# First layer's grouped attention: key blocks stored and loaded by SyncE, both halves in one transfer, and the first turn's operands fetched early

## The reference

```
q = (h @ Wq.T)                              # 32 heads of 128
k_r0 = h @ Wkr.T                            # the rotary part of 8 key heads
c_kv = h @ Wdk.T                            # latents, 512 wide
k_c = c_kv @ Wupk.T ; v = c_kv @ Wupv.T     # the other key part, the values
q, k = q*cos + rotate_half(q)*sin, k*cos + rotate_half(k)*sin
scores = q @ k.T / sqrt(128), causal ; attn = softmax(scores)
out = (attn @ v) @ Wo.T                     # 4 query heads share a key head
```

## Time and profile before

| what | value |
|---|---|
| median of 3 runs | 2360.93 us (2348.55 to 2364.01) |
| the profiled execution | 2363.39 us, its span 2361.7 us |
| granted TensorE clock, mean | 0.959 of full |
| PE busy | 2153.1 us, 91% of the span |
| attn0b, key/value stage after the latents | 405.84 to 516.46 us |
| attn0b, first scores | 540.36 us |

### The profile page before, as it was taken

The page is one execution under the profiler, slowest core; times in us unless marked ns, Lnnn a source line. Parts: engine busy times, 40 slices in busy tenths (PEclk is TensorE's granted clock), DMA queues, the critical chain, the costliest instruction groups (busy, mean ns, idle before and its releaser), DMA issues. The chain is left out here.

```text
span 2361.7 us, 33423 instructions
## 1 busy us (share of the span) xinstructions
PE 2153.1 (91%) x11504; PEld 1480.1 (63%) x11504; DVE 1414.9 (60%) x2599; ACT 1093.5 (46%) x2639; POOL 840.2 (36%) x1062
## 2 busy tenths in 40 slices
PE   6999998887999999999997869999999986899988
PEld 4344366665777777777775656777777664554457
DVE  5777575416566556565663645666666555757756
ACT  4666653214444444444443535555555533325553
POOL 2000000534444444443442025555544412346621
PEclk9899999997999999999999979999999997989999
DMA  2000023651111111111110244433333201543310
GB/s 89 1 1 1 1 76 111 139 118 52 41 54 32 41 54 32 41 32 32 36 50 31 67 103 108 108 91 100 92 98 78 78 23 53 160 95 68 71 34 36
DMA packets 112542, 149.18 MB, mean 63 GB/s; under 512 B 39588, under 2 KB 52516, under 8 KB 110200
## 3 DMA queue, kind: packets, MB, share of 16 engines
q1 hardware_dynamic: 64376, 108.77, 16.3%
q0 software_dynamic: 48000, 38.28, 7.1%
HBM read 86.07 MB, written 27.26 MB: 48 GB/s over the span
## 5 line engine op out<-in xcount | busy, mean ns | idle before, releaser
L1842 POOL TENSOR_TENSOR attn0b_probs<-attn0b_probs,attn0b_recip 128x128 f32<-128x128 f32 (+3 forms) x256 | 192.5, 772 | 223.4 <-DVE attn0b_recip L2081 223.2
L2473 POOL TENSOR_TENSOR attn1a_probs<-attn1a_probs,attn1a_recip 128x128 f32<-128x128 f32 (+3 forms) x256 | 179.2, 721 | 232.9 <-DVE attn1a_recip L2656 232.3
L2529 ACT ACTIVATE attn1a_probs<-attn1a_scores,attn1a_negmax 128x128 f32<-128x128 f32 (+3 forms) x256 | 132.8, 524 | 174.5 <-DVE attn1a_negmax L2642 173.3
L1948 ACT ACTIVATE attn0b_probs<-attn0b_scores,attn0b_negmax 128x128 f32<-128x128 f32 (+3 forms) x256 | 132.8, 524 | 149.5 <-DVE attn0b_negmax L2074 148.3
L1956 ACT ACTIVATE attn0b_probsT<-attn0b_turned 128x128 f32<-128x128 f32 (+3 forms) x128 | 56.0, 438 | 245.7 <-PE attn0b_turned L2222 245.3
L2235 PE MATMUL attn0b_out<-attn0b_probsT,attn0b_v_now 128*128 128x512 f32 x320 | 155.6, 617 | 11.8 <-DVE attn0b_probsT L2088 11.8
L1468 DVE TENSOR_REDUCE attn0a_negmax<-attn0a_by_query 128x2 f32<-128x1024 f32 x128 | 152.3, 1219 | 21.3 <-PE attn0a_by_query L1555 21.3
L2642 DVE TENSOR_REDUCE attn1a_negmax<-attn1a_scores 128x2 f32<-128x256 f32 (+3 forms) x128 | 105.5, 824 | 70.6 <-PE attn1a_scores L2831 70.6
L2074 DVE TENSOR_REDUCE attn0b_negmax<-attn0b_scores 128x2 f32<-128x256 f32 (+3 forms) x128 | 104.8, 819 | 46.5 <-PE attn0b_scores L2211 46.5
L37 PE MATMUL attn0b_aux<-attn0b_wo_hi,attn0b_oT_hi 128*128 128x512 f32 x256 | 126.4, 494 | 1.4 <-DVE attn0b_oT_lo L2092 1.4
L2843 PE MATMUL attn1a_turned<-ident_f,attn1a_probs 128*128 128x128 f32 x640 | 115.8, 279 | 8.6 <-DVE attn1a_probsT L2650 7.2
(11 more groups left out here) (510 smaller groups left out, 6115.0 us busy)
## 6 DMA issues: line engine op xcount, KB each, us to landing
pre<-in_b_o SPq DMA_DIRECT2D x16, 1024.0 KB, 5.3
attn1a_qT<-attn1a_stage SPq DMA_DIRECT2D x128, 128.0 KB, 2.4
attn1a_qT<-attn1a_stage SPq DMA_DIRECT2D x64, 256.0 KB, 3.8
pre<-in_b_q SPq DMA_DIRECT2D x8, 1024.0 KB, 6.4
pre<-in_b_kv SPq DMA_DIRECT2D x5, 1024.0 KB, 5.8
attn0b_vals<-attn0b_v_out SPq DMA_DIRECT2D x16, 256.0 KB, 4.0
attn0b_keys_hi<-attn0b_part_hi POOLq DMA_DIRECT2D x32, 128.0 KB, 5.1
attn0b_keys_lo<-attn0b_part_lo POOLq DMA_DIRECT2D x32, 128.0 KB, 7.7
```

Of the source, the lines that this page charges most:

```text
L1842: pool.tensor_tensor(x, x, recip[:, r % 2, e:e + 1].broadcast_to([P, (qt + 1) * P]), ALU.mult).then_inc(s_scaled, 1)
L1948: act.activation(probs[:, r % 2, e, 0:width], scores[r % 2][:, e, 0:width], ACT.Exp, bias=negmax[:, r % 2, e:e + 1], accum_out=sums[:, r % ...
L2473: pool.tensor_tensor(x, x, recip[:, r % DEEP, e:e + 1].broadcast_to([P, (qt + 1) * P]), ALU.mult).then_inc(s_scaled, 1)
L2529: act.activation(probs[:, r % DEEP, e, 0:width], scores[r % 2][:, e, 0:width], ACT.Exp, bias=negmax[:, r % 2, e:e + 1], accum_out=sums[:, ...
```

## The change

Keys are kept in device memory in one tensor with both halves next to each other; a key part lies in one buffer `part`, of which there are three (`SLOTS`). SP stores it, hi and lo together, in two transfers in place of four, from 64 partitions each; the target is two heads by 64 rows by 512. SP also loads the keys of each turn, with two transfers in place of four. POOL issues none of these any more. SP loads the values of turn 0 after V10 and the keys of turn 0 after V12, inside the key/value stage, and the buffers are laid out anew so that these targets are free by then. The output weights of turn 0 are split at N4, not at `at == 1`. Weights 3 are split one block earlier, at R7. At `at == 0` ACT and DVE wait for all key stores too.

```diff
--- before.py
+++ after.py
     LEAD = 5
+    SLOTS = 3
     FIRST, LAST = -LEAD, TILES_ALL + 1
...
-        keys_hi, keys_lo = [dram(f"keys_{k}", (TURNS, 2, 2, 32, BATCH * SEQ), F32R) for k in ("hi", "lo")]
+        keys = dram("keys", (TURNS, 2, 2, 32, 2, BATCH * SEQ), F32)
             take_sb = lambda name, shape, dt=F32: first.enter_context(nc.sbuf_tensor(f"{prefix}_{name}", shape, dt))
+            part = take_sb("part", [P, SLOTS, 2, SEQ], F32R)
+            v_out = take_sb("v_out", [P, 2, DIM])
             w_hi, w_lo = take_sb("w_hi", [P, 2, KT, DIM], F32R), take_sb("w_lo", [P, 2, KT, DIM], F32R)
...
-            part_hi, part_lo = take_sb("part_hi", [P, 2, SEQ], F32R), take_sb("part_lo", [P, 2, SEQ], F32R)
-            v_out = take_sb("v_out", [P, 2, DIM])
+        probsT = n.sb("probsT", [P, 2, QT, G, P])
+        qT_hi, qT_lo = n.sb("qT_hi", [P, G, BATCH, SEQ], F32R), n.sb("qT_lo", [P, G, BATCH, SEQ], F32R)
+        probs = n.sb("probs", [P, 2, PAIRS, SEQ])
+        oT_hi, oT_lo = n.sb("oT_hi", [P, 2, G, P], F32R), n.sb("oT_lo", [P, 2, G, P], F32R)
         q_cos, q_sin = n.sb("q_cos", [P, 2, SEQ]), n.sb("q_sin", [P, 2, SEQ])
...
-        kT_hi, kT_lo = n.sb("kT_hi", [P, BATCH, SEQ], F32R), n.sb("kT_lo", [P, BATCH, SEQ], F32R)
+        q_raw = n.sb("q_raw", [P, SEQ])
+        n.sb("end_of_latents", [P, 3 * SEQ])
+        kT = n.sb("kT", [P, 2, BATCH, SEQ], F32R)
         v_now = n.sb("v_now", [P, BATCH, QT, HD])
+        wo_hi, wo_lo = n.sb("wo_hi", [P, G, DIM], F32R), n.sb("wo_lo", [P, G, DIM], F32R)
+        wq_hi, wq_lo = n.sb("wq_hi", [P, KT, G, HD], F32R), n.sb("wq_lo", [P, KT, G, HD], F32R)
...
-        s_keys = [n.sem("keys_even"), n.sem("keys_odd")]
+        s_keys = [n.sem(f"keys{k}") for k in range(SLOTS)]
...
+        def stored_until(part):
+
+            return [32 * len([at for at in range(part + 1) if at % SLOTS == k]) for k in range(SLOTS)]
...
+            def store_keys(f):
+                at = PART[f]
+                half, (mt, b) = 0 if f[0] == "R" else 1, divmod(f[1], BATCH)
+                sp.wait_ge(s_plo, at + 1)
+                for s in range(2):
+                    sp.dma_start(keys[2 * mt:2 * mt + 2, s, half, :, :, bass.ts(b, SEQ)],
+                                 part[64 * s:64 * s + 64, at % SLOTS, :, :].bitcast(F32)).then_inc(s_keys[at % SLOTS], 16)
+
+            def store_values(x):
+                half, t = divmod(x, TILES)
+                sp.wait_ge(s_v, x + 1)
+                sp.dma_start(vals[t, :, bass.ts(half, DIM)], v_out[:, x % 2, :]).then_inc(s_vals[x % 2], 16)
+
+            def load_keys(i, b):
+                if i >= 1:
+                    sp.wait_ge(s_scores, PAIRS * (TILES * (i - 1) + QT * (b + 1)))
+                sp.dma_start(kT[:, :, b, :].bitcast(F32),
+                             keys[i].rearrange("s h r p t -> (s h r) p t")[:, :, bass.ts(b, SEQ)]).then_inc(s_kload[b], 16)
+
             for x in range(2, KV_WEIGHTS):
                 load_weights(x)
-            for at in range(16):
-                half, t = divmod(at, TILES)
-                if at == TILES:
+            for f in kinds:
+                if f[0] == "V":
+                    store_values(f[1])
+                if f == ("V", 7):
+                    store_keys(("R", 7))
                     load_queries(0)
                     load_outputs(0)
-                sp.wait_ge(s_v, at + 1)
-                sp.dma_start(vals[t, :, bass.ts(half, DIM)], v_out[:, at % 2, :]).then_inc(s_vals[at % 2], 16)
-            for k in range(2):
-                sp.wait_ge(s_vals[k], 16 * 8)
-            sp.wait_ge(s_proj, len(kinds))
-            for i in range(TURNS):
+                elif f[0] == "V" and f[1] < 7:
+                    store_keys(("R", f[1]))
+                elif f[0] == "N":
+                    store_keys(f)
+                if f == ("V", 10):
+                    for stored in s_vals:
+                        sp.wait_ge(stored, 16 * 4)
+                    for b in range(BATCH):
+                        load_values(0, b)
+                elif f == ("V", 12):
+                    for k in range(SLOTS):
+                        sp.wait_ge(s_keys[k], stored_until(PART["N", 1])[k])
+                    for b in range(BATCH):
+                        load_keys(0, b)
+            for stored in s_vals:
+                sp.wait_ge(stored, 16 * 8)
+            for k in range(SLOTS):
+                sp.wait_ge(s_keys[k], stored_until(15)[k])
+            load_queries(1)
+            load_outputs(1)
+            for i in range(1, TURNS):
+                load_keys(i, 0)
                 load_values(i, 0)
                 if i + 1 < TURNS:
                     load_queries(i + 1)
+                load_keys(i, 1)
+                if i + 1 < TURNS:
                     load_outputs(i + 1)
                 load_values(i, 1)
         def _(pool):
-            def store_keys(f):
-                at = PART[f]
-                kind, (mt, b) = f[0], divmod(f[1], BATCH)
-                half = 0 if kind == "R" else 1
-                for part, keys, done_by in ((part_hi, keys_hi, s_phi), (part_lo, keys_lo, s_plo)):
-                    pool.wait_ge(done_by, at + 1)
-                    for s in range(2):
-                        pool.dma_start(keys[2 * mt:2 * mt + 2, s, half, :, bass.ts(b, SEQ)],
-                                       part[64 * s:64 * s + 64, at % 2, :]).then_inc(s_keys[at % 2], 16)
-
...
                 if f[0] == "R":
                     add_key(f)
-                    if PART[f] >= 1:
-                        store_keys(ROT_BLOCKS[PART[f] - 1])
-                if f[0] == "N":
-                    store_keys(ROT_BLOCKS[PART[f] - 1])
-            store_keys(ROT_BLOCKS[-1])
-            for k in range(2):
-                pool.wait_ge(s_keys[k], 16 * 4 * 8)
-
-            def load_keys(i, b):
-                if i >= 1:
-                    pool.wait_ge(s_scores, PAIRS * (TILES * (i - 1) + QT * (b + 1)))
-                for kT, keys in ((kT_hi, keys_hi), (kT_lo, keys_lo)):
-                    pool.dma_start(kT[:, b, :], keys[i].rearrange("s h r t -> (s h r) t")[:, bass.ts(b, SEQ)]).then_inc(
-                        s_kload[b], 16)
...
-            load_keys(0, 0)
-            load_keys(0, 1)
             for at in range(FIRST, LAST + 1):
                 c = at + LEAD
-                if at >= 0 and at % TILES == QT and at // TILES + 1 < TURNS:
-                    load_keys(at // TILES + 1, 0)
-                if at >= TILES and at % TILES == 0 and at // TILES < TURNS:
-                    load_keys(at // TILES, 1)
...
-                if at >= 2:
-                    act.wait_ge(s_keys[at % 2], 16 * 4 * (at // 2))
-                act.activation(part_hi[:, at % 2, :], full, ACT.Copy).then_inc(s_phi, 1)
+                if at >= SLOTS:
+                    act.wait_ge(s_keys[at % SLOTS], 32 * (at // SLOTS))
+                act.activation(part[:, at % SLOTS, 0, :], full, ACT.Copy).then_inc(s_phi, 1)
...
-                elif f == ("V", 7):
+                        output_weights_hi(0, j)
+                elif f == ("R", 7):
                     split_weights(3)
                 elif f == ("N", 0):
...
                 if at == 0:
                     for stored in s_vals:
                         act.wait_ge(stored, 16 * 8)
+                    for k in range(SLOTS):
+                        act.wait_ge(s_keys[k], stored_until(15)[k])
...
-                if at >= 0 and at % TILES == 1 and at // TILES < TURNS:
+                if at >= TILES and at % TILES == 1 and at // TILES < TURNS:
...
-                dve.tensor_tensor(part_lo[:, at % 2, :], full, part_hi[:, at % 2, :].bitcast(F32),
+                dve.tensor_tensor(part[:, at % SLOTS, 1, :], full, part[:, at % SLOTS, 0, :].bitcast(F32),
                                   ALU.subtract).then_inc(s_plo, 1)
...
             for f in kinds:
                 if f == ("R", 0):
                     split_weights(2)
-                elif f == ("V", 7):
+                elif f == ("R", 7):
                     split_weights(3)
                 elif f == ("N", 0):
                     key_lo(("R", 7))
                     split_weights(4)
+                elif f == ("N", 4):
+                    for j in range(G):
+                        output_weights_lo(0, j)
...
                 if at == 0:
                     for stored in s_vals:
                         dve.wait_ge(stored, 16 * 8)
+                    for k in range(SLOTS):
+                        dve.wait_ge(s_keys[k], stored_until(15)[k])
...
-                    pe.wait_ge(s_kload[b], 32 * (i + 1))
+                    pe.wait_ge(s_kload[b], 16 * (i + 1))
                 pe.wait_ge(s_qlo, BATCH * G * i + G * b + 2 * p + 2)
```

(47 more changed lines are left out.)

## The result

The changed kernel takes 2418.79 us, median of 4 runs (2415.23 to 2420.74), against 2362.47 (2348.55 to 2367.4) before: ratio 1.0249, 95% interval 1.0219 to 1.0279. The range of 2385 to 2435 holds it, and the forecast of 2412 is 7 us low. The profiled execution has a span of 2413.5 us, 51.8 more than before.

What follows compares the result with a forecast made beforehand. PE, busy 91% of the span, was taken as the bound. Key-store wait +53.1, output weights −4.5, restart +2, query weights +1 gave +51.6 us on the profiled 2363.4, so 2415, or 2412 on the median; range 2385 to 2435.

Steps and rivals of the forecast that it cites:

- Two engines a store: SP's key stores, outer count 2, use two of 16 DMA engines: 50.5 GB/s, 10.38 us a part; chance 0.80.
- The length of the row of stores: Key stores and other transfers take 185.0 us on two engines; last key lands at 600.9, delaying the first maximum 53.1 us.
- All else hidden by the wait: In the key/value stage, savings of 25 and 9.7 us fall inside the key-store wait and count nothing; queries ready before 600.
- Output weights, −4.5: Turn 0: taking the output-weight splits away from `at == 1` saves 4.5 us, between 2 and 6.8.
- Restart +2: After the key-store wait, PE has idled some 10 us and restarts at half clock: +2 us (0 to 2.5).
- the late query weights +1: Turn 1's query weights, issued by SP only after all key stores, land at about 607: +1 us (0 to 2).
- The key loads of the steady turns, 0: Turns 1 to 7: SP loading keys in place of POOL changes nothing, between −2 and +2 us for all seven.
- POOL's stores "spread in another way": Kernel before: all 16 parts stored within 117 us, so POOL's transfers use engines differently from SP's; no size given.
- the rival: SP's key stores spread over at least four engines or so, no buffer is waited for: −34.7 us, 2326 us; chance 0.12.

Runs made afterwards that it cites:

- e1: The changed kernel with keys laid out in device memory so that a key store's target is 128 rows in one step (outer count 128); 2329.76 us.
- e4: The changed kernel with its own layout but a key store for each head, four transfers a part in place of two; 2322.14 us.
- e2: The changed kernel with padded rows in device memory, key-store target of outer count 8, and keys loaded in four transfers in place of one; 2334.18 us.
- e3: The changed kernel with padded rows in device memory, key-store target of outer count 4, and key loads in four transfers; 2358.51 us.
- e7: e4 with the output weights of turn 0 split at `at == 1` again; ratio to before 0.9845.
- e8: The kernel before with one edit: SP issues its key stores, shape unchanged (outer count 2), behind the value stores in place of POOL; 2429.8 us.
- e6: e4 with the keys of turns 1 to 7 loaded by POOL again, at its old places; 2337.98 us.
- e10: The kernel before with the key rows of two heads behind each other in device memory, POOL still issuing the stores; 2346.12 us.
- e9: The kernel before with key stores issued by SP and the key rows of two heads behind each other in device memory; 2340.63 us.

## Why the prediction was right, and where it was not

**Two engines a store: right.** Rows of a neighbouring kernel part, with outer counts 8 and 128, were enough to read the count of 2: the share is 0.13. e1 and e4 change the count with the bytes and the queue held, and e2 and e3, whose loads change too, show the shares of 8 and 4 engines. The Trainium skill's rule ("DMA: Bandwidth & Descriptors", "Why a DMA increments its semaphore by 16 and not by 1") agrees with the traces at 2 (0.13), 4 (0.26) and 8 (0.50 and 0.52), and at 4 on the source's side too (e1).

**The length of the row of stores: 6.5 us short** (193.0 for 186.5). The pair was summed as 10.38 + 0.65 = 11.03 us, and the one above takes 11.53: over 16 such pairs that would be 8 us. The windows show why in part: 39 to 51 GB/s while key stores run alone, where 50.5 were taken throughout.

**All else hidden by the wait: right for the stage, but barely.** The first query came 50.7 us late from V0, and the queries were ready at 608, not "before 600"; DVE then waited 2.88 us for the last landing. Stores some 3 us quicker would have left the queries as the last to come. That ACT waits first for key buffers I had; that from V10 on it waits for value stores (six times, 15.4 us at most) I had the other way round. It did not change the sum.

**Output weights, −4.5: the sign right, the size too large;** e7 gives −3.0.

**Restart +2 and the late query weights +1: not borne out.** PE did not idle for the 10 us ahead of the maximum: it was busy 6.65 of the 11 us from 600 on. Its clock was half behind the maximum (0.50 from 612 to 618), as forecast, but a longer turn 0 did not follow. It is as long as e4's (84.4 and 84.3 us), which has no such wait, and in e8, the kernel before with a long row of stores, it is 1.5 us shorter than in the kernel before (88.3 and 89.8). Of the −5.4 us here −3.0 (e7) and −1.2 (e6) are explained. So the two terms together were at most −1 in place of +3; why the last us is gained stays open.

**The key loads of the steady turns, 0: wrong.** I looked at POOL's share and not at what stands directly behind its issues. They cost PE 1.1 us in each turn, with one longer turn of 94.0 some 8 us in all, outside my ±2.

**POOL's stores "spread in another way": right as far as their pace goes, but I drew too little from it.** The forecast took the rival's gain to come from SP; e10 shows that the 30 us between V0 and the first maximum (142.0 to 111.9) lay in the shape on POOL's queue already. Of the change's own edits only the key loads off POOL (about 9 us with turn 0, e6) and the output weights (3 us, e7) show a gain: e9, which has neither the third buffer nor the early loads and splits, reaches the first maximum 1.0 us sooner than e4. The rival's 2326 us for stores that spread is what e1 (2330) and e4 (2322) give.

## What to carry to other kernels

Before a store is moved to another queue, write down its target as the program sees it, outer step first, and read the DMA share of a transfer with that outer count; a share of 0.13 says that 14 of 16 engines stand idle, however long the queue is. The cheapest remedy is the layout in device memory, or a transfer for each outer step, and neither needs another queue. Where an engine that issues transfers also computes for the critical path, look at the instruction right behind its issues, not at how busy it is.
